# Window attention and a shift-and-blur convolution: query and key stacks built through memory outside the chip instead of by copies inside it

## What is computed

```python
x = x + L0(gn(x), w_qkv, w_proj, b_proj, bias_table, rel_index)
x = x + L1(gn(x), offset)
# gn: group norm, 32 groups of 6 channels, no affine part
# L0: attention inside windows of 7 x 7 positions, 12 heads of 16 channels
qkv = einsum('bchw,oc->bohw', x, w_qkv)         # split into windows, heads
dots = q @ k.T * 16 ** -0.5 + bias_table[rel_index]
out = softmax(dots) @ v
out = einsum('bchw,oc->bohw', out, w_proj) + b_proj
# L1: each of 8 groups of 24 channels is shifted by a rounded offset (zeros
# outside), then blurred with a 5 x 5 Gaussian of the remaining offset
```

## Time and profile before

| | |
|---|---|
| median of 3 runs (lowest, highest) | 6754.12 us (6752.31, 6755.74) |
| profiled execution, its own time | 6760.54 us |
| its span, first to last instruction | 6758.8 us |
| busy: PE, DVE, ACT, POOL | 4955.8, 5226.7, 4669.7, 3211.1 us |
| granted TensorE clock, mean | 0.888 |

### The profile page before, as it was taken

The page is one execution under the profiler, slowest core; times in us unless marked ns, Lnnn a source line. Parts: engine busy times, 40 slices in busy tenths (PEclk is TensorE's granted clock), DMA queues, the critical chain, the costliest instruction groups (busy, mean ns, idle before and its releaser), DMA issues.

```text
span 6758.8 us, 233050 instructions
## 1 busy us (share of the span) xinstructions
PE 4955.8 (73%) x81476; PEld 3795.1 (56%) x81476; DVE 5226.7 (77%) x11722; ACT 4669.7 (69%) x15619; POOL 3211.1 (48%) x3428
## 2 busy tenths in 40 slices
PE   5777777877777777778777777767787777777776
PEld 4555555655555555556555555555565555555554
DVE  4888777887778887778877788877787777878784
ACT  3777666776667776667766677766677666777673
POOL 1355444554445554445544455544455444555454
PEclk9998889988889988889888899988898888989897
DMA  3545556455555455554555554555545555545554
GB/s 80 111 102 116 112 115 121 102 114 114 112 118 118 104 116 113 115 121 101 116 115 111 117 120 103 115 113 114 121 104 114 115 110 117 119 102 112 114 111 76
DMA packets 1368966, 750.78 MB, mean 111 GB/s; under 512 B 1182938, under 2 KB 1256666, under 8 KB 1363546
## 3 DMA queue, kind: packets, MB, share of 16 engines
q1 hardware_dynamic: 1367770, 735.06, 52.6%
HBM read 156.66 MB, written 154.14 MB: 46 GB/s over the span
## 4 chain that ended last, share of the span: by engine, by line
SPq 27%; DVE 21%; PE 17%; issue 14%; POOL 7%; ACT 6%; DMA 5%; DVEq 1%; POOLq 0%; ACTq 0%
SPq L390 9%; SPq L384 6%; DMA xt<-in_x 4%; SPq L454 4%; SPq L421 4%; ACT prob L774 3%; DVE den L980 3%; DVE pT L989 3%; SPq L403 3%; PE pTr L571 3%; POOL probn L1191 2%; DVE qks L942 2%; DVE mx L966 2%; PE pO L589 2%; DVE mix L942 2%
## 5 line engine op out<-in xcount | busy, mean ns | idle before, releaser
L1191 POOL TENSOR_TENSOR probn<-prob,den 128x588 f32<-128x588 f32 x1024 | 1199.9, 1172 | 2512.4 <-DVE den L985 2348.5
L589 PE MATMUL pO<-pT,vv 98*32 98x49 f16 x36864 | 772.6, 212 | 1312.1 <-DVE pT L989 889.7
L774 ACT ACTIVATE prob<-pS,mx 128x49 f32<-128x49 f32 x4096 | 1178.7, 305 | 600.3 <-DVE mx L965 589.3
L589 PEld LDWEIGHTS pO<-pT,vv 98*32 98x32 f16 x36864 | 666.6, 138 | 1534.6 <-DVE pT L989 822.4
L989 DVE SCALAR_TENSOR_TENSOR pT<-pTr,pT 98x588 f16<-98x588 f32 x1024 | 754.7, 737 | 839.4 <-DMA xt<-in_x 374.8
L571 PE MATMUL pTr<-cst,probn 128*98 128x128 f32 x6144 | 987.6, 303 | 22.1 <-POOL probn L1191 21.5
L787 ACT ACTIVATE pT<-pTr 98x588 f16<-98x588 f32 x1024 | 684.2, 668 | 426.3 <-PE pTr L571 422.1
L774 ACT ACTIVATION_READ_ACCUMULATOR prob<-pS,mx 128x1 f32 x4096 | 853.1, 208 | 0.0
L552 PE MATMUL pS<-biasT,addb 128*64 128x196 f16 (+1 forms) x4096 | 602.0, 324 | 258.6 <-ACT prob L774 191.2
L571 PEld LDWEIGHTS pTr<-cst,probn 128*98 128x98 f32 x6144 | 714.2, 140 | 56.2 <-POOL probn L1191 29.2
L559 PE MATMUL pS<-kst,qst 96*64 96x98 f16 x12288 | 690.5, 221 | 0.0
(11 more groups left out here) (186 smaller groups left out, 14841.7 us busy)
## 6 DMA issues: line engine op xcount, KB each, us to landing
kst<-qks SPq DMA_DIRECT2D x1536, 98.0 KB
qst<-qks SPq DMA_DIRECT2D x1536, 49.0 KB, 1.9
kst<-mix SPq DMA_DIRECT2D x768, 98.0 KB
vv<-cv SPq DMA_DIRECT2D x1024, 73.5 KB
out<-xr SPq DMA_DIRECT2D x256, 294.0 KB
xr<-x_scratch SPq DMA_DIRECT2D x64, 882.0 KB
x_scratch<-xm SPq DMA_DIRECT2D x128, 392.0 KB, 3.0
xm<-in_x SPq DMA_DIRECT2D x32, 1176.0 KB, 14.9
```

Source lines behind the costliest of these rows:

```text
L589: mm = pe.matmul(pO[r:r + 32, p % 2, hp // 4, NT * win:NT * win + NT], vv[:, g % 2, win, p % PPR, a, hp::NHP], pT[0:98, p % 2, b, 2 * hp + ...
L774: a = act.activation(prob[:, p % 2, t], pS[:, 0, t], ACT.Exp, bias=mx[:, p % 2, h:h + 1], scale=-1.0, accum_out=den[:, p % 2, h:h + 1])
L1191: pool.tensor_tensor(heads(probn[:, p % 2, :]), heads(prob[:, p % 2, :]), spread(den[:, p % 2, :], NT), ALU.mult).then_inc(S["norm_p"], 1)
```

## The change

Each block is written once to a tensor in DRAM (`spill`), already in the order of the stack, and read back from there into `qst` or `kst` (`stack`). The source of a doubled part is read with a step of zero. The DRAM tensors are `q_spill`, `k_spill` and `t_spill` with two slots each, of 128 rows x 3 parts. A row of the stack is then 3 x (row of the head pair) + part instead of 32 x part + row, in `qst` and `kst` alike. Per chunk there are 2 + 2 + 4 transfers out and 1 + 1 + 2 back. The transfer back waits for the one out. `spill` stands in SP's program where `stack` stood, `stack` one pair later (`late`, p = P+2, P+4, P+6). ACT's wait before it overwrites `qks` or `mix` is now for the spill.

```diff
-            def stack(i, c, blk):
-                buf, done = c % 2, S[("stack_q", "stack_k", "stack_t")[blk]]
+            def spill(i, c, blk):
+                buf = c % 2
                 sp.wait_ge(S["qk_dve"], nth("qk_dve", i, 6 * c + 2 * blk + 2))
                 if blk != 1:
-                    src = qks if blk == 0 else mix
-                    for n, hp in enumerate(range(4) if blk == 0 else range(4, NHP)):
-                        for r, part in enumerate((0, 1, 0) if blk == 0 else (0, 2, 0)):
-                            sp.dma_start(qst[32 * r:32 * r + 32, buf, CHUNK * hp:CHUNK * hp + CHUNK],
-                                         src[32 * n:32 * n + 32, part, :]).then_inc(done, 16)
+                    src, dst, rows, done = (qks, qd, 128, S["spill_q"]) if blk == 0 else (mix, td, 64, S["spill_t"])
+                    lo = 1 if blk == 0 else 2
+                    hi = src[0:rows, 0, :].rearrange("p (o t) -> p o t", o=1).to_broadcast([rows, 2, CHUNK])
+                    sp.dma_start(dst[buf, 0:rows, 0:3:2, 0:CHUNK], hi).then_inc(done, 16)
+                    sp.dma_start(dst[buf, 0:rows, 1, 0:CHUNK], src[0:rows, lo, :]).then_inc(done, 16)
                 if blk != 0:
...
+                    sp.dma_start(dst[buf, a:b, 0:2, :], hi.to_broadcast([b - a, 2, 2 * CHUNK])).then_inc(done, 16)
+                    sp.dma_start(dst[buf, a:b, 2, :], both[:, 2 * CHUNK:4 * CHUNK]).then_inc(done, 16)
+
+            def stack(i, c, blk):
+                buf = c % 2
+                if blk != 1:
+                    src, n, done = (qd, 4, S["stack_q"]) if blk == 0 else (td, 2, S["stack_t"])
+                    if blk == 0:
+                        sp.wait_ge(S["spill_q"], nth("spill_q", i, 32 * (c + 1)))
+                    else:
+                        sp.wait_ge(S["spill_t"], nth("spill_t", i, 64 * (c + 1)))
+                    at = 0 if blk == 0 else 4 * CHUNK
+                    sp.dma_start(qst[:, buf, at:at + n * CHUNK].rearrange("p (n t) -> p n t", n=n),
+                                 src[buf, 0:32 * n, :, 0:CHUNK].rearrange("(n p) r t -> (p r) n t", n=n)
+                                 ).then_inc(done, 16)
+                if blk != 0:
+                    src, row, n, hp, done = (kd, 0, 4, 0, S["stack_k"]) if blk == 1 else (td, 64, 2, 4, S["stack_t"])
+                    if blk == 1:
+                        sp.wait_ge(S["spill_k"], nth("spill_k", i, 32 * (c + 1)))
+                    sp.dma_start(kst[:, buf, hp:hp + n, :, :].rearrange("p n e t -> p n (e t)"),
+                                 src[buf, row:row + 32 * n, :, :].rearrange("(n p) r t -> (p r) n t", n=n)
+                                 ).then_inc(done, 16)
...
             def body(i, prev, att, nxt):
                 for p in range(PAIRS):
                     qk = before(qk_step, p, prev, att, nxt)
                     if qk and qk[2] % 2:
+                        spill(i + qk[0], qk[1], qk[2] // 2)
+                    qk = late(qk_step, p, prev, att, nxt)
+                    if qk and qk[2] % 2:
                         stack(i + qk[0], qk[1], qk[2] // 2)
```

More of the change, by code:

```diff
@@ L127, with build @@
 SET_HOT, SET_GAUSS, SET_ALL = 5, 23, 42
-def build(nc, x, w_in, b_out, table, rel, offset, cf, ch, scratch, out):
+def build(nc, x, w_in, b_out, table, rel, offset, cf, ch, scratch, qd, kd, td, out):
     images = x.shape[0]
@@ L212, in build @@
             "const_in", "setup", "setup_act", "setup_pe",
-            "x_in", "x1_out", "xr_in", "y_out", "stack_q", "stack_k", "stack_t", "vst0", "vst1",
+            "x_in", "x1_out", "xr_in", "y_out", "spill_q", "spill_k", "spill_t", "stack_q", "stack_k", "stack_t", "vst0", "vst1",
             "gn1_bn", "gn2_bn", "gn1_dve", "gn1_pe", "gn1_pool", "gn2_dve", "gn2_pe", "gn2_pool",
@@ L220, in build @@
             "c1_pe", "z_act", "z_dve", "c2_pe", "y_dve")}
-        PER = {"x_in": 64, "x1_out": 128, "xr_in": 64, "y_out": 8 * 16, "stack_q": 192 * NCH,
-               "stack_k": 192 * NCH, "stack_t": 192 * NCH, "gn1_bn": 12, "gn2_bn": 12, "gn1_dve": 8, "gn1_pe": 2, "gn1_pool": 2,
+        PER = {"x_in": 64, "x1_out": 128, "xr_in": 64, "y_out": 8 * 16, "spill_q": 32 * NCH, "spill_k": 32 * NCH, "spill_t": 64 * NCH, "stack_q": 16 * NCH,
+               "stack_k": 16 * NCH, "stack_t": 32 * NCH, "gn1_bn": 12, "gn2_bn": 12, "gn1_dve": 8, "gn1_pe": 2, "gn1_pool": 2,
                "gn2_dve": 13, "gn2_pe": 3, "gn2_pool": 1, "xnh_a": 16, "xnl_p": 8,
@@ L310, in before, with late @@
             return (last[0] - 1, *last[1:]) if last else None
+        def late(step, p, prev, att, nxt):
+            if p >= 2:
+                return step(p - 2, att, nxt)
+            last = step(PAIRS + p - 2, prev, att)
+            return (last[0] - 1, *last[1:]) if last else None
         def tail_bank(r):
@@ L735, in qk_hi @@
                 act.wait_ge(S["qk_pe"], nth("qk_pe", i, 6 * c + g + 1))
[L737 to L742, removed]
+                if g == 0 and due("spill_q", i, 32 * c):
+                    act.wait_ge(S["spill_q"], nth("spill_q", i, 32 * c))
+                if g == 2 and due("spill_k", i, 32 * c):
+                    act.wait_ge(S["spill_k"], nth("spill_k", i, 32 * c))
+                if g == 4 and due("spill_t", i, 64 * c):
+                    act.wait_ge(S["spill_t"], nth("spill_t", i, 64 * c))
                 blk, t = g // 2, slice(ROW * (g % 2), ROW * (g % 2) + ROW)
@@ L1216 @@
     scratch = nc.dram_tensor("x1_scratch", (C, TOK), F32, kind="Internal").ap()
+    qd, kd, td = (nc.dram_tensor(n, (2, 128, 3, size), F16, kind="Internal").ap()
+                  for n, size in (("q_spill", CHUNK), ("k_spill", 2 * CHUNK), ("t_spill", 2 * CHUNK)))
     out = nc.dram_tensor("out_0", x.shape, F32, kind="ExternalOutput").ap()
-    build(nc, *aps, scratch, out)
+    build(nc, *aps, scratch, qd, kd, td, out)
     r = run(nc, [arrays], core_ids=[0])
```

16 lines of the change are left out of this document (7 added, 9 removed).

## The result

The changed kernel takes 7146.16 us (median of 4 runs, 7139.53 to 7216.95), beside 6754.93 us for the kernel before: a ratio of 1.060, 95% interval 1.053 to 1.067. It is 391 us slower, 13 us for each of the 30 passes, where 207 us less were forecast. The span of the profiled execution is 7137.8 us, 379 us longer.

A forecast was written before the change was run, and what follows sets the result against it. SP's issuing and, at the start of a pass, the DMA engines were taken to bound the kernel in turns. 5.4 - 0.5 + 2 = 6.9 us a pass, 30 passes, 207 us, gave 6547 us; range 6400 to 6840.

The forecast's parts named there:

- The rival on the slower side: DMA engines take the gain back at 235 GB/s, at pass starts and chunk ends: 6850 us, chance 0.24.
- SP is held in other places: Rings behind the read of `xr` hold SP at new transfers too, 6.5 us more: no gain, 6754 us, chance 0.10.
- The sign that the prediction named for being wrong: At the chunks' ends, PE's wait for the t block growing to 3 us or more.
- the gain of 5.4 us a pass: Start of a pass: DVE has x at 3034.8 instead of 3040.2, 5.4 us earlier.
- the values by 3014.1: Start of a pass: SP has issued the values by 3014.1; they land at 3016.3, against 3017.6.
- the end of the pass gains 2 us: End of a pass: values behind one round trip of keys, 7.4 us instead of 8 to 10; gain 2 us.
- 10.7 us: Chunk ends: t's trip through DRAM, from data ready to landing, with nothing between, 10.7 us against 11.3 for copies.
- 300 GB/s for both legs: Rate assumed for the stacks' data out to DRAM and back: 300 GB/s, 3.3 us a MB.
- a copy writes 32 partitions, a new transfer 64 to 128: Argument on the stacks' DMA rate, for leaning to the store's 361 GB/s over the keys' copies' 235.
- the rest of x 5 us for 1.2 MB: Start of a pass: x's last 1.2 MB takes 5 us, since two halves write 64 partitions each; landed at 3034.8.
- I count nothing for the first such place: Chunk ends at p = 21 and 29: no loss at the first (no output), 0.5 us at the second.
- The share of the transfer queue: Whole kernel: the DMA engines' busy share should rise from 52.6% to 65 to 70%.

The follow-up runs named there:

- q_only: The changed kernel with only the queries' block through DRAM, keys and t copied inside SBUF as before: 6571.19 us, ratio 0.975.
- v_first: The changed kernel, but SP issues the values' four transfers before the keys' way back instead of after it: 6919.23 us, ratio 1.026.
- k_only: The changed kernel with only the keys' block through DRAM, queries and t copied inside SBUF: 7117.49 us, ratio 1.056.
- k_vfirst: As k_only, but SP issues the values' four transfers before the keys' way back: 6618.7 us, ratio 0.977.
- t_only: The changed kernel with only the t block through DRAM, queries and keys copied inside SBUF: 7055.12 us, ratio 1.047.
- wide: The changed kernel with the way back of queries and keys into 128 partitions, three rows each, instead of 96 with four: 6966.76 us, ratio 1.033.

## Why the prediction was wrong

**The sign and the size.** Forecast 6547 us, range 6400 to 6840, measured 7146. The rival on the slower side ended at 6850. It had the right place (chunk ends) and, for the way back, nearly the rate (about 250 GB/s), but the way out ran at 400, the engines were not full, and its loss of some 100 us is a quarter of what was measured. "SP is held in other places" came nearest to the mechanism. It looked for the hold at the keys' spill, where none came, and priced it at nothing. The sign that the prediction named for being wrong, a wait of PE for t of 3 us or more, was met with 4.4.

**The start of a pass, right for the queries.** The read of `xr` was issued when the forecast had it, and the gain of 5.4 us a pass that follows from it is near what `q_only` shows: 5.9 us in one pass, 4.2 in the median. In the whole change t and keys took it back before x: in the last row of the table DVE has x 0.5 us later than in the kernel before, over all passes 1.8 us (medians 60.9 and 59.1).

**The failed step: "the values by 3014.1".** I gave the values' four transfers the 3.4 us that they take behind small copies. The rows beside them showed SP held for 7.6 us at the read of `xr` and for 6.6 behind it, and I had used just that there, but not for the keys' way back. The values' issue behind it took 6.7 to 7.2 us, at each of the four chunks of a pass. At the start of the pass they landed 2.2 us after their issue ended, as before: what they lost is time of SP. No run takes the hold alone away. Issuing the values first, which also takes them from behind SP's wait for the keys' spill, is worth 227 us in the changed kernel (`v_first`) and 499 us with the keys alone (`k_only`, `k_vfirst`). The same step was behind "the end of the pass gains 2 us" and behind t's late start.

**The mis-sized term: "10.7 us" for t.** It was counted from the data being ready, where the copies took 11.3, so I forecast a trip 0.6 us shorter than theirs. Counted from the first issue it is 12.0 us with nothing between, against 10.3 for the copies: 1.7 us longer. At one place of `t_only`, with the output between, it is 14.8 (3038.6 to 3053.4). The spill landed 3.7 us after its last issue where I had 2.7, the way back took 5.3 where I had 4.3. For the second the rate is the likely reason: 300 GB/s for both legs was 400 out and 250 back, as the keys' stretches show. The one difference in form that I weighed, "a copy writes 32 partitions, a new transfer 64 to 128", led me to the faster row. Yet my own sum gave the rest of x 5 us for 1.2 MB, 240 GB/s, because its halves write 64 partitions; the way back into 96 needed the same thought.

**The neglected bound.** PE waited 1 us for t at half of all chunk ends. I read that as a small cost. It was a sign that the path had hardly any slack there, so that a lengthening of t's trip by 1.7 us could not be hidden; "I count nothing for the first such place" assumed a cover that wasn't there.

**A term put at nothing.** The sum has no price for the clock. With PE's longer waits the granted clock fell, and PE was busy 220 us longer for the same instructions (182 us longer with t alone through DRAM). How much of the 391 us that makes stays open.

**What was right.** The share of the transfer queue (65 to 70% forecast, 65.5 measured). The fit on the Trainium skill's page "DMA: Bandwidth & Descriptors", section "Anatomy of one DMA", is given there for transfers that GpSimd issues; here SP issues them. For a spill of 0.4 MB it gives 2.9 us, and the queries' spill has a median of 2.7. For 1.2 MB it gives 4.8 us; the way back landed after 7.4 us in 96 partitions and after 5.5 in `wide`, so here the measurement decides against it.

## What to carry to other kernels

Count for each transfer not only when it lands but what is issued behind it on the same queue: small transfers with an urgent reader belong ahead of a large one, and with the keys alone through DRAM their order was worth more (499 us) than the loss of the whole change (391). A wait that is short but stands at many places can mark a path without slack; here t's longer route showed in full. A longer route pays where its reader has time (in the kernel after, queries issued at 3096.5 land some 7 us later and are needed at 3126) and costs where the reader waits already (t).

## What the runs showed of the hardware

- The issue of a transfer on SP's queue is not a constant. Four transfers of 73.5 KB (392 runs each) took 3.4 us behind small copies, 6.7 to 7.5 us behind one transfer of 1.2 MB into 96 partitions, 5.6 us behind a way out of 1.2 MB from 128 partitions, 4.8 us behind four of 0.3 MB, and once 10.1 us behind the load of x and the keys' spill (`v_first`, 3068.4). Copies of 32 runs were not held behind the same 1.2 MB.
- 1.2 MB from DRAM: about 250 GB/s into 96 partitions in runs of 3136 bytes, up to 442 into 128 in runs of 9408, at about the same share of the 16 engines. The way out from 128 partitions in runs of 3136 ran at 400. The first load of x moved 452 GB/s into 128 partitions in runs of 3136, 213 into 64 in runs of 6272. Why fewer partitions are slow was not tried.
- TensorE's granted clock fell to 0.50 while TensorE stood idle for 4.8 us waiting for t (kernel after, 0.50 from 3130 to 3140). In the same place of the kernel before, where it had waited 1 us, it stayed at 1.00.
- Copies inside SBUF to partitions three apart cost what copies to adjacent ones cost (ratio 0.999, 0.998 to 1.000).
